# Batch 0 of the attention: first projection of batch 1 moved up behind unit 2 on its own signal, the plan of tiles moved to the end

## The chip, the cores and the metric

The kernel runs on one core of one Trainium2 chip. The metric is the device time of one execution in microseconds (us), median of several runs. TensorE, VectorE, ScalarE and GpSimd each work through a queue of instructions in the order in which they were written; SyncE issues most of the transfers. They meet only at semaphores: an instruction waits until a counter has reached a value. The profile calls the engines PE, DVE, ACT, POOL and SP.

## The reference, cut to what matters

```
xn  = layernorm(x)                                  # x: 16 batches of 512 tokens, 128 wide
q, k, v = xn@Wq, xn@Wk, xn@Wv                       # 16 heads, 8 wide
attn = softmax(causal(8 * l2norm(q) @ l2norm(k).T)) # per batch and head
attention = (attn @ v) @ Wo
probs = softmax(xn @ Wr.T); the 2 best of 8 experts, their shares made to sum to 1
ffn  = sum over the 2 of share * (gelu(xn @ W1[e].T + b1[e]) @ W2[e].T + b2[e])
out  = x + attention + ffn
```

## The kernel before

**Stages.** First every batch is normalised, turned and stored, and the experts of all tokens are chosen. Then the attention of batches 0 to 7 runs, then 71 tiles of the expert layer (each 256 tokens of one expert), then the attention of batches 8 to 15. GpSimd sends the rows of normalised tokens to their places in the experts' tiles (`slot_x`) with indirect transfers while the first eight batches run, and fetches the results during the later ones.

**One batch of attention.** `body` of TensorE goes through 12 units, k = 0 to 11. In unit k `scores` (L911 to L925) writes 1,536 columns of scores into one of two areas of PSUM, ScalarE raises them to exp (L813, one instruction each unit), GpSimd sets the masked ones to zero (`mask`, L666, one or two instructions in each unit), and `weigh` (L957, L968) multiplies the result by the values, in ten chunks c = 0 to 9. `scores` of unit k waits until the exp of unit k-2 is over, because it uses its area. `weigh` of chunk 0 starts the sums in PSUM bank 6 (`ps_o`); chunks 0 to 4 are the first half of the heads, chunks 5 to 9 the second. Between them VectorE must empty the bank: `evacuate` (L1361), then `divide` (L1367, L1371). Chunk 4 needs the masks of unit 6, chunk 6 those of unit 7, chunk 7 those of unit 9; the last two chunks follow in the next batch.

**Projections.** Among the units TensorE also makes q, k and v of the next batch, tile by tile: `project(b + 1, i)` (L883) for i = 0 to 3, all four into PSUM bank 7. VectorE takes each one out (`prepare`: `unload`, L1228 and L1235, then `halve`, L1244 to L1252), and `project` of the next tile waits for L1235 (the counter `proj_evac`). SyncE then turns each tile into place for the next batch's scores (L432).

**What is special in batch 0.** VectorE is still at work on the routing when batch 0 begins. From the ranks that TensorE left in bank 7 (`ps_pc`) it works out the slot of each token: L1326 and L1327 read the bank, L1328 to L1334 work on in SBUF, L1337 clears bank 6, and then it raises the counter `routed`. Three things wait for `routed`: `project(1, 0)`, because it overwrites bank 7; `weigh` of chunk 0, because of bank 6 and the buffers there; and GpSimd's first send. GpSimd's queue in batch 0 is written out by hand: masks of units 0 to 5, then a wait for `routed` and for the transfer that fills the last tiles with zeros (L625), one send, mask 6, two sends, mask 7, one send, mask 8, two sends, mask 9, one send, mask 10, one send, mask 11. VectorE in batch 0 prepares the four tiles of batch 1, then does `pick_tiles` (L1342 to L1345, the table of which expert owns which tile, needed by TensorE only in unit 7 of batch 1), then `evacuate` and `divide` of the first half.

The order of TensorE in batch 0: scores 0, 1, 2, 3; `project(1, 0)`; scores 4; chunks 0 and 1; scores 5; `project(1, 1)`; scores 6; chunk 2; `project(1, 2)`; scores 7, 8; chunk 3; `project(1, 3)`; chunk 4; scores 9, 10; chunks 5 and 6; scores 11; chunk 7.

Of the kernel before, what the change touches and what calls it, by code (L numbers as in the profile page):

```python
# [29 lines left out]
def build(nc, x, Wq, Wk, Wv, Wo, Wr, W1, b1, W2_, b2, out):  # L30
# [3 lines left out]
    TB = N // P  # L34
# [64 lines left out]
    with ExitStack() as ctx:  # L99
# [3 lines left out]
        def sem(name):  # L103
            return ctx.enter_context(nc.semaphore(name))

        def sems(names):
            return [sem(n) for n in names.split()]
# [145 lines left out]
        wtr_done, wt_ready, btr_done, bt_ready = sems("wtr_done wt_ready btr_done bt_ready")  # L253
        r_step, counted, totals_read, placed = sems("r_step counted totals_read placed")
        routed = sem("routed")
        residue_ready, later_ready = sems("residue_ready later_ready")
        gap_exp, = sems("gap_exp")
        pick_ready, picked, plan_ready = sems("pick_ready picked plan_ready")
# [13 lines left out]
        def some(count):  # L272


            return not isinstance(count, int) or count > 0
# [6 lines left out]
        def known(i, value):  # L282

            return isinstance(i, int) and i == value
# [5 lines left out]
        def tile_of(b, i):  # L290

            return i if known(b, 0) else TILE_AT[i]
# [542 lines left out]
        def _(pe):  # L835
# [35 lines left out]
            def project(b, i):  # L871

                t = tile_of(b, i)
                if i == 0:
                    pe.wait_ge(xt_in, 16 * (b + 1))
                if not known(b, 0):
                    if i == 0 and known(b, 1):
                        pe.wait_ge(routed, 1)
                    if i == 0 and some(b - 2):
                        pe.wait_ge(added, b - 2)  # L880
                    pe.wait_ge(proj_evac, TB * b + i)
                bank = psum[:, t, :] if known(b, 0) else psum[:, 7, :]
                pe.matmul(bank[:, 0:3 * D], xt[:, t * P:(t + 1) * P], wall[:, E:WEND], start=True, stop=True)\  # L883
                    .then_inc(proj_done, 1)
# [90 lines left out]
            def out_project(b, projected):  # L975
                pe.wait_ge(ot_ready, b + 1)
                pe.wait_ge(proj_evac, projected)
                for t in range(TB):
                    mm = pe.matmul(ps_out[:, t * D:(t + 1) * D], ot[:, t * P:(t + 1) * P], wo[:],  # L979
                                   start=True, stop=True)  # L980
                mm.then_inc(outp_done, 1)
# [34 lines left out]
            pe.wait_ge(bt_ready, 1)  # L1016
            pe.wait_ge(proj_evac, TB)

            def body(b, par, second=False, last=False):
                if known(b, HALF):  # L1020
                    pe.wait_ge(gelu_done, MC * FFN_TILES)
                    pe.wait_ge(ys_ready, FFN_TILES)
                fresh = known(b, 0) or known(b, HALF)
                for k in range(UN):
                    scores(b, par, k)
                    if k == 1 and not last and not known(b, 0):
                        project(b + 1, 0)
                    elif k == 2 and not fresh:
                        weigh(b - 1, 1 - par, 8)
                        weigh(b - 1, 1 - par, 9)  # L1030
                    elif k == 3 and not last:
                        project(b + 1, 0 if known(b, 0) else 1)
                    elif k == 4:
                        weigh(b, par, 0)
                        weigh(b, par, 1)
                    elif k == 5 and not last:
                        project(b + 1, 1 if known(b, 0) else 2)
                    elif k == 6:
                        weigh(b, par, 2)
                        if not last:  # L1040
                            project(b + 1, 2 if known(b, 0) else 3)
                    elif k == 7 and known(b, 1):
                        pe.wait_ge(pick_ready, 1)
                        pe.wait_ge(proj_evac, TB * (b + 2))
                        pe.matmul(ps_pick, pick[:], identh[:, 0:FFN_TILES], start=True, stop=True).then_inc(picked, 1)
                    elif k == 8:
                        weigh(b, par, 3)
                        if known(b, 0):
                            project(b + 1, 3)
                        weigh(b, par, 4)  # L1050
                    elif k == 9:
                        if known(b, 1):
                            pe.wait_ge(wo_in, 16 * 4 * QH)
                            pe.wait_ge(plan_ready, 1)
                        if not known(b, 0):
                            out_project(b - 1, TB * (b + 1) if last else TB * (b + 2))
                    elif k == 10:
                        weigh(b, par, 5)
                        weigh(b, par, 6)
                    elif k == 11:  # L1060
                        weigh(b, par, 7)
# [48 lines left out]
        def _(dve):  # L1110
# [91 lines left out]
            def next_step():  # L1202

                nonlocal steps
                steps += 1
                return steps
# [51 lines left out]
            def share_values(b, par):  # L1258

                if known(b, 0):  # L1260
                    dve.wait_ge(vp_made, 3)
                dve.wait_ge(proj_evac, TB * (b + 1))
                first = v[0:HP, par].rearrange("p (m j) x -> p j m x", j=2)[:, 0, :, 0:DH]
                dve.tensor_copy(vp[0:HP, par, :, 0:DH], first)
                other = v[0:HP, par].rearrange("p (m j) x -> p j m x", j=2)[:, 1, :, 0:DH]
                dve.tensor_copy(vp[HP:P, par, :, DH + 1:2 * DH + 1], other).then_inc(vp_ready, 1)
# [16 lines left out]
            def stepped(ins):  # L1283
                ins.then_inc(r_step, 1)
                dve.wait_ge(r_step, next_step())
# [38 lines left out]
            def of_halves(ap):  # L1324
                return ap.rearrange("p h (a e) -> p h a e", a=1).broadcast_to([P, 2, T // 2, E])
            dve.tensor_tensor(ahead, ranks, of_halves(upto[:, 1:3]), ALU.is_ge)  # L1326
            stepped(dve.tensor_tensor(at_rank, ranks, of_halves(begins[:, 0:2]), ALU.add))  # L1327
            stepped(dve.tensor_tensor(ahead, ahead, of_halves(jumps[:]), ALU.mult))  # L1328
            stepped(dve.tensor_tensor(at_rank, at_rank, ahead, ALU.add))
            for c in range(TOPK):  # L1330
# [10 lines left out]
            def pick_tiles():  # L1341
                stepped(dve.tensor_scalar(past[:], ends[:].rearrange("p c e -> p (c e)"), tile_at[:], None, ALU.is_le))  # L1342
                stepped(dve.tensor_tensor(past[:], past[:], weight[:], ALU.mult))
                stepped(dve.tensor_reduce(expert[:], past[:], AX.X, ALU.add))
                dve.tensor_scalar(pick[:], ones[:], expert[:], None, ALU.mult).then_inc(pick_ready, 1)  # L1345
# [60 lines left out]
            def body(b, par, second=False, last=False):  # L1406
                fresh = known(b, 0) or known(b, HALF)

                if known(b, 0):
                    share_values(0, 0)  # L1410
                if not (second or known(b, HALF)):
                    scale_of(b + 1, rnb[:])
                if not last:
                    prepare(b + 1, 1 - par, 0, second)
                if not fresh:
                    evacuate(b - 1, 1)
                if last:
                    divide(b - 1, 1)
                    turn_divided(b - 1)
                else:  # L1420
                    prepare(b + 1, 1 - par, 1, second)
                    if not fresh:
                        divide(b - 1, 1)
                    prepare(b + 1, 1 - par, 2, second)
                    if not fresh:
                        turn_divided(b - 1)
                    prepare(b + 1, 1 - par, 3, second)
                if known(b, 0):
                    pick_tiles()
                if known(b, 1):  # L1430
                    write_plan()
                evacuate(b, 0)
                divide(b, 0)
                if not last:
                    share_values(b + 1, 1 - par)
                if not known(b, 0):
                    add_attention(b - 1)
                if second and not known(b, HALF):
                    added_before = counted_by(dve, b)
                    dve.wait_ge(made, 1)  # L1440
                    dve.wait_ge(added, added_before)
                    combine(b - 1, 1 - par, range(MOVES))
                if last:
                    combine(b, par, range(2))
# [151 lines left out]
```

## Time and profile before

| | |
|---|---|
| time, median of 3 runs | 667.08 us (666.76 to 668.74) |
| the profiled execution: its own time | 667.76 us |
| its span, first to last instruction | 666.0 us |
| mean granted clock of TensorE | 0.971 of full speed |
| busy: TensorE, VectorE, ScalarE, GpSimd | 607.1, 461.8, 450.5, 427.2 us |

Times in the rows are microseconds from the start of the span; batch 0 lies between about 88 and 117. A row of the timeline gives start, duration, engine, line, operation, what it writes from what it reads, and in brackets how long the engine stood idle before it and what ended that.

### The profile page before, as it was taken

What the parts mean: (1) busy time and instruction counts of PE and PEld (TensorE: products, weight loads), DVE (VectorE), ACT (ScalarE), POOL (GpSimd) and SP (SyncE); (2) the same over time, 40 slices, a digit from 0 to 9 for tenths busy, and PEclk for the clock granted to TensorE, in tenths of its full rate; (3) what the DMA queues carried; (4) which work ended last, traced back from release to release, by engine and by line L of the source; (5) the groups of instructions that cost most, each with busy time, mean ns of one, the idle gap of its engine ahead of it and who ended that gap; (6) DMA issues with size and microseconds to landing.
All of it is one profiled execution on the core that took longest, in us unless ns stands there. A gap on an engine that the chain in (4) does not pass through costs nothing.

```text
span 666.0 us, 21498 instructions
## 1 busy us (share of the span) xinstructions
PE 607.1 (91%) x7417; PEld 411.3 (62%) x7417; DVE 461.8 (69%) x1296; ACT 450.5 (68%) x689; POOL 427.2 (64%) x617
## 2 busy tenths in 40 slices
PE   2877468999999989999999999999998999989985
PEld 2756322444444448999999999999994444434432
DVE  6799986677777776444444546777666688868846
ACT  3999546789898984444444444444457988978893
POOL 6356627778888887775600026777655777868773
PEclk9999868999999999999999999999999999989998
DMA  6997684445664568745332334444434466555541
GB/s 172 286 289 243 191 251 107 102 105 122 117 129 112 126 129 218 203 136 145 111 87 71 79 86 107 119 117 115 118 97 75 101 125 135 125 118 111 127 109 48
DMA packets 186593, 89.37 MB, mean 134 GB/s; under 512 B 115456, under 2 KB 176032, under 8 KB 186400
## 3 DMA queue, kind: packets, MB, share of 16 engines
q1 hardware_dynamic: 178192, 70.70, 43.8%
q0 software_dynamic: 8336, 17.84, 9.7%
q8 instruction: 36, 0.59, 0.4%
q14 instruction: 29, 0.24, 0.1%
HBM read 30.17 MB, written 32.24 MB: 94 GB/s over the span
## 4 chain that ended last, share of the span: by engine, by line
PE 74%; issue 4%; DVE 4%; ACT 4%; POOL 3%; DMA 2%; SPq 0%; DVEq 0%; ACTq 0%; POOLq 0%
PE psum L1085 19%; PE psum L1073 18%; PE psum L968 14%; PE psum L883 7%; PE psum L911 7%; ACT prob L813 2%; PE psum L918 2%; PE psum L957 2%; PE psum L979 2%; DMA xt<-xn_cols 2%; POOL prob L666 1%; PE psum L925 1%; POOL rows L650 1%; ACT prob L766 1%; POOL slot_x L652 1%
## 5 line engine op out<-in xcount | busy, mean ns | idle before, releaser
L813 ACT ACTIVATE prob<-psum 128x1536 f32<-128x1536 f32 x192 | 266.9, 1452 | 51.2 <-PE psum L911 47.7
L823 ACT ACTIVATE prob<-psum,prob 128x256 f32<-128x256 f32 x284 | 117.5, 471 | 132.9 <-PE psum L1073 130.1
L650 POOL DMA_INDIRECT rows<-slot_y,idx x128 | 131.4, 1026 | 45.9 <-issue 26.3
L652 POOL DMA_INDIRECT slot_x<-rows,slots x128 | 128.1, 1001 | 35.5 <-issue 29.4
L666 POOL TENSOR_SCALAR_AFFINE_SELECT prob<-prob 128x128 f32<-128x128 f32 (+2 forms) x256 | 112.8, 455 | 42.8 <-ACT prob L813 39.4
L1085 PEld LDWEIGHTS psum<-prob 128*128 128x128 f32 x1136 | 137.8, 192 | 3.6
L968 PE MATMUL psum<-prob,v 128*18 128x448 f32 (+3 forms) x2048 | 132.5, 388 | 7.9 <-POOL prob L666 7.7
L1085 PE MATMUL psum<-prob 128*128 128x128 f32 x1136 | 138.1, 275 | 0.0
L1073 PE MATMUL psum<-xs,prob 128*128 128x256 f32 x568 | 134.8, 380 | 0.9 <-DVE xs L1475 0.8
L1073 PEld LDWEIGHTS psum<-xs,prob 128*128 128x128 f32 x568 | 102.5, 190 | 12.8 <-issue 1.2
L968 PEld LDWEIGHTS psum<-prob,v 128*18 128x18 f32 x2048 | 50.4, 99 | 79.4 <-issue 57.9
L911 PE MATMUL psum<-qks 32*128 32x192 f16 (+3 forms) x1024 | 67.6, 275 | 4.3 <-ACT prob L813 4.1
L1482 DVE TENSOR_TENSOR xs<-psum,prob 128x256 f32<-128x256 f32 x71 | 30.1, 424 | 58.6 <-PE psum L1085 58.4
L883 PE MATMUL psum<-wall,xt 128*128 128x384 f32 x128 | 58.8, 544 | 4.0 <-issue 2.9
L911 PEld LDWEIGHTS psum<-qks 32*128 32x128 f16 x1024 | 20.7, 92 | 55.9 <-issue 25.4
L1459 DVE COPY prob<-wexp 128x516 f32 x71 | 31.6, 446 | 32.7 <-ACT prob L823 30.0
L1467 DVE COPY prob<-wexp 128x640 f32 x71 | 35.6, 502 | 14.6 <-DVE xs L1482 14.6
L635 POOL COPY idx<-slots 128x8 int32 (+1 forms) x16 | 3.5, 217 | 64.1 <-PE psum L1085 63.8
L1403 DVE SCALAR_TENSOR_TENSOR acc<-rows,gate,acc 128x128 f32<-128x128 f32 (+1 forms) x128 | 42.4, 395 | 3.0 <-DMA rows<-slot_y,idx 1.6
L1361 DVE STREAM_TRANSPOSE turn<-psum 128x512 f32<-128x512 f32 x31 | 22.2, 715 | 21.0 <-PE psum L968 21.0
L846 PE MATMUL psum<-wall,xts 128*128 128x264 f32 x128 | 32.0, 397 | 4.5 <-ACT logits L767 4.5
L1228 DVE TENSOR_TENSOR qn<-psum,rnb 128x256 f32<-128x256 f32 x36 | 14.8, 412 | 28.4 <-PE psum L883 28.3
(159 smaller groups left out, 676.5 us busy)
## 6 DMA issues: line engine op xcount, KB each, us to landing
slot_y<-xs SPq DMA_DIRECT2D x71, 128.0 KB
xs<-in_L_attn_x SPq DMA_DIRECT2D x16, 256.0 KB, 4.1
prob<-in_L_ffn_W SPq DMA_DIRECT2D x16, 256.0 KB, 3.6
xn_rows<-prob SPq DMA_DIRECT2D x16, 256.0 KB, 2.6
xn_cols<-xts SPq DMA_DIRECT2D x16, 256.0 KB, 3.0
xt<-xn_cols SPq DMA_DIRECT2D x16, 256.0 KB
rows<-xn_rows SPq DMA_DIRECT2D x16, 256.0 KB, 3.1
out<-acc SPq DMA_DIRECT2D x15, 256.0 KB
```

The costliest lines, as they stand in the source:

```text
L650: pool.indirect_dma_start(rows[:, j, c, t, :], None, done, where).then_inc(moved[j], 16)
L652: pool.indirect_dma_start(slot_x, where, halves_of_rows[:, j, 0, t, :], None).then_inc(moved[j], 16)
L666: pool.affine_select(out=p, in_=p, compare_op=ALU.is_ge, fill=0.0, base=HP, pattern=[[0, n], [0, 2], [1, HP]], channel_multiplier=-1).then ...
L813: act.activation(prob[:, KEPT[k], :], score[k % 2], ACT.Exp, scale=SCALE / UP ** 2)\
L823: act.activation(hs[:, s, c, :], psum[:, 2 * s + c // 2, (c % 2) * FT:(c % 2 + 1) * FT], ACT.Gelu, bias=ws[:, s, B1C + c:B1C + c + 1]).the ...
L883: pe.matmul(bank[:, 0:3 * D], xt[:, t * P:(t + 1) * P], wall[:, E:WEND], start=True, stop=True)\
L911: mm = pe.matmul(s[:, j * N + col:j * N + col + cols], keys, queries(qks[g:g + 32, par, 0, slab], kt, first, cols), start=True, stop=True)
L968: mm = pe.matmul(queries(ps_o[32 * g:32 * g + VW], kt, first, cols), pairs[par][:, kt * H // 2 + QH * o + g, odd:odd + VW], prob[:, KEPT[u ...
L1073: mm = pe.matmul(psum[:, 2 * s + c // 2, (c % 2) * FT:(c % 2 + 1) * FT], ws[:, s, c * P:(c + 1) * P], xgt[:, s, :], start=True, stop=True)
L1085: mm = pe.matmul(psum[:, 4 + s, j * D:(j + 1) * D], hs[:, s, c, j * P:(j + 1) * P], ws[:, s, W2C + c * D:W2C + (c + 1) * D], start=(c == 0 ...
L1403: dve.scalar_tensor_tensor(out=a, in0=r, scalar=gate[:, c, at(TB * m + t)], in1=a, op0=ALU.mult, op1=ALU.add).then_inc(combined, 1)
L1467: dve.tensor_copy(ws[:, s:s + 1, W2C:WX], wexp[:, at(e), W2C:WX]).then_inc(w2_ready, 1)
```

## The change

A second counter, `ranks_read`, is raised by VectorE as soon as L1327 has read bank 7; `project(1, 0)` waits for it in place of `routed`. In batch 0 TensorE follows a list of its own (`entry`): scores 0, 1, 2; `project(1, 0)`; scores 3, 4, 5; chunks 0 and 1; `project(1, 1)`; scores 6; chunk 2; `project(1, 2)`; scores 7, 8; `project(1, 3)`; chunks 3 and 4; scores 9, 10; chunks 5 and 6; scores 11; chunk 7. VectorE does `evacuate`, `divide` and `share_values` of batch 0 before `pick_tiles`. The same work is done; the queues of GpSimd, ScalarE and SyncE and the other batches keep their order.

```diff
+        ranks_read = sem("ranks_read")
...
                 if not known(b, 0):
                     if i == 0 and known(b, 1):
-                        pe.wait_ge(routed, 1)
+                        pe.wait_ge(ranks_read, 1)
...
+            def entry(k):
+
+                if k == 2:
+                    project(1, 0)
+                elif k == 5:
+                    weigh(0, 0, 0)
+                    weigh(0, 0, 1)
+                    project(1, 1)
+                elif k == 6:
+                    weigh(0, 0, 2)
+                    project(1, 2)
+                elif k == 8:
+                    project(1, 3)
+                    weigh(0, 0, 3)
+                    weigh(0, 0, 4)
+                elif k == 10:
+                    weigh(0, 0, 5)
+                    weigh(0, 0, 6)
+                elif k == 11:
+                    weigh(0, 0, 7)
...
                 for k in range(UN):
                     scores(b, par, k)
-                    if k == 1 and not last and not known(b, 0):
+                    if known(b, 0):
+                        entry(k)
+                        continue
+                    if k == 1 and not last:
                         project(b + 1, 0)
...
                     elif k == 3 and not last:
-                        project(b + 1, 0 if known(b, 0) else 1)
+                        project(b + 1, 1)
...
             stepped(dve.tensor_tensor(at_rank, ranks, of_halves(begins[:, 0:2]), ALU.add))
+            dve.sem_inc(ranks_read, 1)
             stepped(dve.tensor_tensor(ahead, ahead, of_halves(jumps[:]), ALU.mult))
...
-                if known(b, 0):
-                    pick_tiles()
                 if known(b, 1):
                     write_plan()
                 evacuate(b, 0)
                 divide(b, 0)
                 if not last:
                     share_values(b + 1, 1 - par)
-                if not known(b, 0):
+                if known(b, 0):
+                    pick_tiles()
+                else:
                     add_attention(b - 1)
```

## Rows read from the trace of the kernel before

**Rows 1.** The page: engines' busy time (us, share, instructions), and the chain that ended last.

```profile
PE 607.1 (91%) x7417; PEld 411.3 (62%) x7417; DVE 461.8 (69%) x1296; ACT 450.5 (68%) x689; POOL 427.2 (64%) x617
...
PE 74%; issue 4%; DVE 4%; ACT 4%; POOL 3%; DMA 2%; SPq 0%; DVEq 0%; ACTq 0%; POOLq 0%
```

**Rows 2.** Chain of waits in order of time: the first scores of batches 2 and 3.

```profile
136.90 0.54 PE psum L918 x2
...
155.22 0.54 PE psum L918 x2
```

**Rows 3.** Timeline of TensorE in batch 0.

```profile
93.67 0.39 PE L911 MATMUL psum<-qks 32*128 32x320 f16 x6 [1.10 <-ACT prob L813]
96.95 1.62 PE L883 MATMUL psum<-wall,xt 128*128 128x384 f32 x2 [2.89 <-issue]
...
101.97 0.91 PE L883 MATMUL psum<-wall,xt 128*128 128x384 f32 x2
...
107.35 1.06 PE L968 MATMUL psum<-prob,v 128*18 128x320 f32 x16
...
111.26 0.68 PE L957 MATMUL psum<-prob,xts 128*18 128x64 f32 x32 [2.31 <-DVE turn L1361]
...
114.78 1.91 PE L968 MATMUL psum<-prob,v 128*18 128x448 f32 x16 [0.59 <-POOL prob L666]
```

**Rows 4.** Timeline of ScalarE in batch 0.

```profile
90.67 5.63 ACT L813 ACTIVATE prob<-psum 128x1536 f32<-128x1536 f32 x4 [6.95 <-PE psum L911]
...
102.09 2.79 ACT L813 ACTIVATE prob<-psum 128x1536 f32<-128x1536 f32 x2 [1.48 <-PE psum L911]
```

**Rows 5.** Timeline of GpSimd in batch 0 and at the start of batch 1.

```profile
91.51 1.21 POOL L625 DMA_INDIRECT slot_x<-acc,pad_at  x1 [7.90 <-issue]
...
104.67 0.98 POOL L652 DMA_INDIRECT slot_x<-rows,slots  x1 [0.16 <-issue]
105.67 0.92 POOL L666 TENSOR_SCALAR_AFFINE_SELECT prob<-prob 128x256 f32<-128x256 f32 x2
...
111.74 1.16 POOL L652 DMA_INDIRECT slot_x<-rows,slots  x1 [0.17 <-ACT prob L813]
...
114.18 0.55 POOL L666 TENSOR_SCALAR_AFFINE_SELECT prob<-prob 128x384 f32<-128x384 f32 x1
...
120.34 0.29 POOL L666 TENSOR_SCALAR_AFFINE_SELECT prob<-prob 128x128 f32<-128x128 f32 x1 [2.19 <-ACT prob L813]
```

**Rows 6.** Timeline of VectorE in batch 0 and at the start of batch 1.

```profile
91.10 0.68 DVE L1327 TENSOR_TENSOR rows<-psum,begins 128x512 f32<-128x512 f32 x1
...
96.30 0.48 DVE L1337 MEMSET psum<- 128x512 f32 x1 [0.18 <-DVE slots L1334]
...
99.22 0.28 DVE L1235 COPY v<-psum 128x128 f32<-128x128 f32 x1
...
109.26 0.51 DVE L1342 TENSOR_SCALAR past<-ends,tile_at 128x24 f32<-128x24 f32 x1
...
110.51 0.70 DVE L1361 STREAM_TRANSPOSE turn<-psum 128x512 f32<-128x512 f32 x1
...
120.58 0.42 DVE L1228 TENSOR_TENSOR qn<-psum,rnb 128x256 f32<-128x256 f32 x1 [6.67 <-PE psum L883]
```

**Rows 7.** Transfers: packets between 83.2 and 88 us.

```profile
DMA packets 2243, 1.13 MB, mean 236 GB/s; under 512 B 1042, under 2 KB 2066, under 8 KB 2243
```

**Rows 8.** Transfers: the one that fills the last tiles, its time to landing (us) last.

```profile
slot_x<-acc,pad_at POOLq DMA_INDIRECT x1, 8.9
```

**Rows 9.** Stretches: busy time of each engine, PEclk the granted clock, DMA share, GB/s.

```profile
93.00:94.00 1.00, 0.33 (x6) 0.12 (x6) 0.93 (x3) 1.00 (x2) 0.64 (x2) 1.00 1.06 293
94.00:95.00 1.00, 0.06 (x3) 0.00 (x0) 0.96 (x2) 1.00 (x2) 0.11 (x1) 0.83 1.18 356
...
118.00:119.00 1.00, 1.00 (x26) 0.35 (x14) 0.00 (x0) 0.23 (x1) 0.15 (x1) 0.72 0.17 66
```

**Rows 10.** Stretches around the end of batch 7, same columns.

```profile
247.00:248.00 1.00, 0.00 (x0) 0.00 (x0) 0.00 (x0) 0.98 (x3) 0.97 (x1) 1.00 0.37 100
```

More of the change, by code:

```diff
@@ L1036, in body @@
                     elif k == 5 and not last:
-                        project(b + 1, 1 if known(b, 0) else 2)
+                        project(b + 1, 2)
                     elif k == 6:
@@ L1040, in body @@
                         if not last:
-                            project(b + 1, 2 if known(b, 0) else 3)
+                            project(b + 1, 3)
                     elif k == 7 and known(b, 1):
@@ L1047, in body @@
                         weigh(b, par, 3)
-                        if known(b, 0):
-                            project(b + 1, 3)
                         weigh(b, par, 4)
@@ L1054, in body @@
                             pe.wait_ge(plan_ready, 1)
-                        if not known(b, 0):
-                            out_project(b - 1, TB * (b + 1) if last else TB * (b + 2))
+                        out_project(b - 1, TB * (b + 1) if last else TB * (b + 2))
                     elif k == 10:
@@ L1427, in body @@
                     prepare(b + 1, 1 - par, 3, second)
-                if known(b, 0):
-                    pick_tiles()
                 if known(b, 1):
@@ L1435, in body @@
                     share_values(b + 1, 1 - par)
-                if not known(b, 0):
+                if known(b, 0):
+                    pick_tiles()
+                else:
                     add_attention(b - 1)
```

## The prediction

> **What bounds the kernel now.** I read the page first. TensorE is busy for 91% of the span, and 74% of the chain that ended last is its work [rows 1]. So the question is what ends batch 0 on TensorE, and whether time won there survives. The chain of waits shows how steady batches run: the first scores of batch 2 start at 136.90, those of batch 3 at 155.22, 18.32 us apart, with nothing but TensorE between them [rows 2].
>
> The timelines of batch 0 show four places where TensorE isn't the limit. It reaches scores 3 at 93.67, and then stands until 96.95, when `project(1, 0)` starts; the brackets count 2.89 us idle [rows 3]. L1337 ends at 96.30 + 0.48 = 96.78, and `routed` comes next: that is the wait [rows 6]. ScalarE runs four exps from 90.67 to 96.30, 1.41 us each, and then has nothing, because the scores of units 4 and 5 stand behind that wait; exps 5 and 6 run from 102.09 to 104.88 [rows 4]. GpSimd is late for the same reason: its first send starts at 104.67, mask 6 at 105.67, mask 9 at 114.18, and there is hardly a gap between; chunk 7 follows at 114.78, and the profile names L666 as its releaser [rows 3, 5]. Last, chunk 5 starts at 111.26, behind `evacuate`, though chunk 4 was over at 107.35 + 1.06 = 108.41 [rows 3]; between the two stood `pick_tiles`, from 109.26 to 110.51, 1.25 us [rows 6]. What ends batch 0 is GpSimd's queue, and what starts that queue late is exp 6, by way of `routed`.
>
> **The change step by step.** Times are those of the old profile up to 92 and worked out from there.
>
> *The first projection.* L1327 ends at 91.78 [rows 6], so the new signal is up at about 91.9. Scores 2 need exp 0 (92.08) and 0.4 us, so `project(1, 0)` starts at 92.5 and doesn't wait for VectorE. Nor for `xt`: its 128 pieces of 2 KB stand ahead of the load of `acc` in SyncE's queue, and 2243 - 2066 = 177 packets of 2 KB or more had passed by 88 us [rows 7]. One projection took 1.62 us at the low clock and 0.91 at the high one [rows 3]; here the clock is high [rows 9], so it ends at 93.4, before scores 3 could start (exp 1 ends at 93.49). It costs the path nothing. If `xt` came later, TensorE would stand in front of scores 3 to 5, and the old order would be back.
>
> *Units 3 to 5.* Their scores wait for exps 1, 2 and 3 (93.5, 94.9, 96.3) and take 0.4 us each [rows 3, 4]. Exps 4 and 5 then follow exp 3 without a gap, and exp 5 ends at 96.30 + 2 x 1.41 = 99.1, where it ended at 102.09 + 1.40 = 103.5 before. Chunks 0 and 1 wait for `routed`, still 96.9. The new signal stands in VectorE's queue ahead of it; no row has its price, which lies between nothing and 0.28, the shortest VectorE instruction in [rows 6]. I take 0.1.
>
> *The second projection is the new limit.* `project(1, 1)` waits for L1235 of tile 0. VectorE reaches that only after the routing and ended it at 99.50 [rows 6]; with the signal, 99.6. Chunks 0 and 1 are through by then: between 98.57 and 101.97 they and two units of scores took 3.40 us at the low clock [rows 3], so without the scores at most 2.6, from 97.0 to 99.6. From 99.6 the projection takes 0.91 or 1.62, scores 6 take 0.4 or, by estimate between that and its double, 0.6, and exp 6 takes 1.40: it ends at 102.3 at the high clock, 103.2 at the low one.
>
> *GpSimd.* Mask 5 follows exp 5 and is over at 100.0 (0.9 us for such a pair, as mask 6). Then GpSimd waits for the fill of the last tiles, issued at 91.51 and landed 8.9 us later, at 100.4 [rows 5, 8]; nothing of the change touches it. The first send (0.98) is over by 101.5, so mask 6 starts with exp 6, at 102.3 to 103.2 instead of 105.67: 3.4 or 2.5 us earlier. From mask 6 to mask 9 it took 114.18 - 105.67 = 8.51 us, the same instructions in the same order, and VectorE was at work beside them then as now. I keep 8.51; the upper bound is five sends at the 1.16 of the slowest one here in place of 0.98, 0.9 more [rows 5]. The Trainium skill speaks against the step here: by its page "SBUF — State Buffer", section "Who interferes with whom", a copy of VectorE in its fast modes shuts GpSimd out from writing the descriptors of a send until it is over. If each of the five sends waited out one copy of 0.28, that would be 1.4 us and the sum below 2.1; the rows agree with 0.18 a send at most. Exps 7 to 9 are in time: from `project(1, 1)` to the end of chunk 4 took 108.41 - 101.97 = 6.4 us [rows 3], so chunk 4 is over at 106.0 to 107.2 and exp 9, which needs its buffer, 1.4 us and a unit of scores later, before 109.1, when mask 9 is due at 110.8 or later. The swap of `project(1, 3)` and chunk 3 moves nothing past another engine's wait.
>
> *The plan of tiles.* Without `pick_tiles` ahead of it, `evacuate` starts up to 1.25 us sooner, around 107 to 108. That is worth nothing at the end, because chunk 7 still waits for mask 9 at 111 or later. Nor does `pick_tiles` cost anything at its new place: VectorE stands idle for 6.67 us before 120.58 [rows 6], and TensorE asks for the result in unit 7 of batch 1. Were that cover gone, it would cost its 1.25 us.
>
> *The clock after it.* Chunk 7 took 1.91 us at half speed, and the clock rose only about 118.5 (0.72 granted in 118 to 119) [rows 3, 9]. If it stays high this time, (118.5 - 114.8) / 2 = 1.9 us come on top; if it falls as before, nothing. TensorE will again stand for about 2 us before chunk 7, as it did for 2.31 before chunk 5, so I take 0.5, near the lower end. Against that, 247 to 248 was a whole microsecond without a matmul, at 1.00 granted [rows 10].
>
> *The sum.* 2.5 to 3.4 us earlier, of which I take 3.0, because TensorE between 93 and 97 is again busy for less than half of the time, and the last time that was so the clock fell inside 94 to 95 [rows 9]; and 0.5 from the clock after it: 3.5 us. It survives: batches 2 to 7 are TensorE's alone [rows 2], GpSimd had 2.19 us of slack at the start of batch 1 [rows 5], and all transfers of batch 1 start from semaphores that move along. The profiled execution took 667.76 us (its span 666.0), so the same one would take 664.3. It lies 0.68 above the median of the runs; from the median of 667.08 it is 663.6, which I give.
>
> **The rivals.** *The clock stays high.* The trace speaks half for it: high at 247 in spite of the gap [rows 10], low from 94 on although scores ran until then [rows 9]. Then mask 6 starts 3.4 us earlier and the tail gives 1.9: 5.3 us, 661.8. [...]
>
> *The gain goes on GpSimd's queue: no change.* The sends stretch, or the fill lands later. Five slow sends (0.9) and the low clock leave 2.5 - 0.9 = 1.6 us: 665.5. For nothing at all, the first send would have to start at 104.67 as before, the fill 4.3 us later than it landed. Against it: sends ran beside a busy VectorE before too.
>
> *Slower, by the clock.* Many short gaps between 93 and 99.6 could keep TensorE at 1.2 GHz where the second projection of the old order already ran at 2.4 (0.91 at 101.97) [rows 3], and again behind chunk 7. A microsecond on TensorE's path at half speed costs 0.5. To use up 3.0 and lose 2.0 more, the low stretches must be 10 us longer than before: low until about 107 and again until 122. Then 669.5. Nothing in the trace lasts so long while TensorE is as busy as from 99.6 on.
>
> **How the numbers follow.** 0.3% of 667 is 2.0 us, about what a measurement of this kernel can tell from no change. The forecast, a gain of 2.0 to 4.6 us, gets 0.59; the high clock 0.15; no change 0.19; slower 0.07. Faster is 0.59 + 0.15 = 0.74, same 0.19, slower 0.07. The forecast's own range is 662.5 to 665.1. The range down to 661.3 takes in the high clock with half a microsecond to spare; up to 666.3 it takes in the stretched sends. What is left out is a gain of under 0.8 us and a loss.
>
> **What would show it.** The first projection should start at 92.5 and scores 3 at 93.5; six exps should run on end from 90.67 to 99.1; `project(1, 1)` should start at 99.6, released by VectorE's L1235; mask 6 should start at 102.3 to 103.2, and chunk 7 at 110.8 to 112.3 with GpSimd still its releaser; the first scores of batch 2 should come 3 to 4 us before 136.90. I am wrong if `project(1, 0)` waits for something else, if mask 6 waits for a send or the fill rather than for exp 6, or if the granted clock is low for longer in sum than before.

## The result and the profile after

The changed kernel takes 665.47 us (median of 20 runs, 663.35 to 668.51); the kernel before took 668.35 on the same chips (20 runs, 666.42 to 672.33). The ratio is 0.9947, 95% interval 0.9931 to 0.9963: faster by 0.53%, or 3.5 us of 668.35, where 3.5 us were forecast; the medians themselves lie 2.9 apart. 665.47 lies 1.9 above the forecast time of 663.6, and 1.3 of that are the kernel before itself, which took 668.35 here and 667.08 in the three runs that the forecast started from.

The profiled execution took 666.04 us, its span is 664.3. Its times can't be set beside those of before as they stand, since this execution came to batch 0 about a microsecond later. As a common mark I take the first matmul of the counts on the routing, which no edit touches: it starts at 87.18 here and started at 86.20 before (L1006 there). "After the mark" is a time less that start. TensorE's timeline in batch 0 of the changed kernel (the lines of the file have moved: `project` is L884, scores L912 to L926, chunks L958 and L969):

```profile
87.18 0.27 PE L1007 MATMUL psum<-residue,xs 128*128 128x8 f16 x4 [0.78 <-DVE xs L1301]
...
92.57 0.39 PE L912 MATMUL psum<-qks 32*128 32x448 f16 x6 [0.62 <-ACT prob L814]
92.92 0.89 PE L884 MATMUL psum<-wall,xt 128*128 128x384 f32 x2
...
96.60 0.41 PE L912 MATMUL psum<-qks 32*128 32x320 f16 x6 [0.95 <-ACT prob L814]
99.02 1.06 PE L958 MATMUL psum<-prob,xts 128*18 128x64 f32 x32 [2.01 <-DVE xts L1288]
...
101.72 1.65 PE L884 MATMUL psum<-wall,xt 128*128 128x384 f32 x2
...
110.16 0.64 PE L958 MATMUL psum<-prob,xts 128*18 128x64 f32 x32 [0.45 <-DVE turn L1384]
...
114.36 1.91 PE L969 MATMUL psum<-prob,v 128*18 128x448 f32 x16 [2.37 <-POOL prob L667]
116.21 1.03 PE L919 MATMUL psum<-barred,identh 128*128 128x512 f16 x2
```

ScalarE's timeline of the same stretch, and GpSimd's:

```profile
91.06 8.17 ACT L814 ACTIVATE prob<-psum 128x1536 f32<-128x1536 f32 x6 [6.35 <-PE psum L912]
103.90 1.45 ACT L814 ACTIVATE prob<-psum 128x1536 f32<-128x1536 f32 x1 [4.67 <-PE psum L912]
```

```profile
92.50 1.21 POOL L626 DMA_INDIRECT slot_x<-acc,pad_at  x1 [7.91 <-issue]
...
101.54 1.01 POOL L653 DMA_INDIRECT slot_x<-rows,slots  x1 [1.51 <-issue]
105.49 0.66 POOL L667 TENSOR_SCALAR_AFFINE_SELECT prob<-prob 128x256 f32<-128x256 f32 x2 [2.95 <-ACT prob L814]
...
113.75 0.56 POOL L667 TENSOR_SCALAR_AFFINE_SELECT prob<-prob 128x384 f32<-128x384 f32 x1
...
119.59 0.29 POOL L667 TENSOR_SCALAR_AFFINE_SELECT prob<-prob 128x128 f32<-128x128 f32 x1 [1.85 <-ACT prob L814]
```

VectorE's:

```profile
92.92 0.69 DVE L1351 TENSOR_TENSOR logits<-logits,jumps 128x512 f32<-128x512 f32 x1 [0.16 <-DVE rows L1349]
...
97.41 0.48 DVE L1360 MEMSET psum<- 128x512 f32 x1 [0.18 <-DVE slots L1357]
...
98.59 0.29 DVE L1288 COPY xts<-v 64x256 f32<-64x256 f32 x1
...
100.50 0.28 DVE L1257 COPY v<-psum 128x128 f32<-128x128 f32 x1
...
111.82 0.24 DVE L1365 TENSOR_SCALAR past<-ends,tile_at 128x24 f32<-128x24 f32 x1
...
119.83 0.42 DVE L1250 TENSOR_TENSOR qn<-psum,rnb 128x256 f32<-128x256 f32 x1 [5.93 <-PE psum L884]
```

And stretches of a microsecond (the busy time of TensorE is the second figure, the granted clock the third from the end):

```profile
95.00:96.00 1.00, 0.39 (x6) 0.12 (x6) 0.93 (x3) 1.00 (x2) 0.76 (x2) 1.00 1.07 293
96.00:97.00 1.00, 0.40 (x6) 0.12 (x6) 0.97 (x2) 1.00 (x2) 0.33 (x1) 0.92 1.12 369
97.00:98.00 1.00, 0.01 (x1) 0.00 (x0) 0.71 (x2) 1.00 (x2) 0.21 (x1) 0.50 1.01 420
...
103.00:104.00 1.00, 1.00 (x11) 0.27 (x14) 0.60 (x3) 0.10 (x1) 0.00 (x0) 0.66 0.86 192
...
117.00:118.00 1.00, 1.00 (x38) 0.58 (x38) 0.00 (x0) 0.00 (x0) 0.72 (x2) 0.84 0.19 70
```

The first projection starts at 92.92, 5.74 after the mark in place of 10.75 [rows 3], and six exps run on end from 91.06. But chunk 0 starts only at 99.02, 2.01 us idle behind L1288, the copy that shares out the values; L1360, behind which `routed` is raised, had ended at 97.89. The clock has fallen in 96 to 97 and the second projection takes 1.65 us, from 101.72. So exp 6 starts at 103.90, mask 6 at 105.49, mask 9 at 113.75, chunk 7 at 114.36, and GpSimd is its releaser as before [rows 3, 5]. After the mark, mask 6 moved from 19.47 to 18.31, chunk 7 from 28.58 to 27.18 and the first scores of batch 1 from 30.43 to 29.03: 1.40 us. The low clock ends at about 117.3, 30.1 after the mark where it was 32.4, and the first scores of batch 2 come 1.7 us earlier.

### The profile page after: what moved, and what is told of

The parts are those of the page before. It is cut to its first block, busy times and chain, and to the rows that moved or that the text cites. A ratio compares the mean times of both kernels' runs of the same rounds, so it can differ in the third digit from the quotient of the medians.

```text
span 664.3 us, 21499 instructions
## 1 busy us (share of the span) xinstructions
PE 605.6 (91%) x7417; PEld 411.8 (62%) x7417; DVE 460.8 (69%) x1296; ACT 450.2 (68%) x689; POOL 428.0 (64%) x617
## 4 chain that ended last, share of the span: by engine, by line
PE 73%; DVE 6%; issue 4%; ACT 3%; POOL 3%; DMA 1%; SPq 0%; DVEq 0%; ACTq 0%; POOLq 0%
PE psum L1107 19%; PE psum L1095 18%; PE psum L969 15%; PE psum L884 7%; PE psum L912 6%; ACT prob L814 2%; PE psum L919 2%; PE psum L958 2%; PE psum L980 2%; POOL prob L667 2%; PE psum L926 1%; POOL rows L651 1%; DMA xt<-xn_cols 1%; POOL slot_x L653 1%; ACT prob L767 1%
## 5 line engine op out<-in xcount | busy, mean ns | idle before, releaser
L969 PE MATMUL psum<-prob,v 128*18 128x448 f32 (+3 forms) x2048 | 130.7, 385 | 9.7 <-POOL prob L667 9.5
L969 PEld LDWEIGHTS psum<-prob,v 128*18 128x18 f32 x2048 | 50.1, 98 | 79.8 <-issue 53.3
L912 PE MATMUL psum<-qks 32*128 32x320 f16 (+3 forms) x1024 | 66.7, 273 | 5.6 <-ACT prob L814 5.2
L1505 DVE TENSOR_TENSOR xs<-psum,prob 128x256 f32<-128x256 f32 x71 | 30.1, 424 | 58.8 <-PE psum L1107 58.7
L884 PE MATMUL psum<-wall,xt 128*128 128x384 f32 x128 | 58.5, 541 | 1.3 <-DMA xt<-xn_cols 0.6
L912 PEld LDWEIGHTS psum<-qks 32*128 32x128 f16 x1024 | 20.6, 92 | 57.0 <-ACT prob L814 25.0
L597 POOL TENSOR_TENSOR rows<-prob 128x512 f32<-128x512 f32 x16 | 20.6, 1288 | 21.3 <-DVE xns L1200 19.6
```

The costliest lines, as they stand in the source:

```text
L912: mm = pe.matmul(s[:, j * N + col:j * N + col + cols], keys, queries(qks[g:g + 32, par, 0, slab], kt, first, cols), start=True, stop=True)
L969: mm = pe.matmul(queries(ps_o[32 * g:32 * g + VW], kt, first, cols), pairs[par][:, kt * H // 2 + QH * o + g, odd:odd + VW], prob[:, KEPT[u ...
```

## The experiments

Each ratio is to the kernel before, on the same chip; its median there lay between 668.35 and 669.35, so rows are compared by their ratios and not by their medians. To keep what happens in batch 0 apart from what happens later, the table gives, for the profiled execution of each, the starts of the first scores of batch 1 and batch 2 after the mark.

| kernel | median, us | ratio (95%) | batch 1 | batch 2 |
|---|---|---|---|---|
| before | 668.35 | 1 | 30.43 | 50.63 |
| changed | 665.47 | 0.9947 (0.9931 to 0.9963) | 29.03 | 48.92 |
| changed, old signal | 669.16 | 0.9990 (0.9972 to 1.0009) | 31.32 | 51.00 |
| changed, plan of tiles first | 666.04 | 0.9956 (0.9934 to 0.9979) | 27.67 | 47.33 |
| before, new signal alone | 665.76 | 0.9961 (0.9937 to 0.9986) | 29.23 | 48.63 |
| changed, sends spread | 661.01 | 0.9884 (0.9849 to 0.9919) | 25.47 | 45.13 |
| before, sends spread | 666.62 | 0.9950 (0.9933 to 0.9967) | 29.46 | 48.85 |
| changed, values shared early | 663.70 | 0.9921 (0.9894 to 0.9947) | 27.47 | 47.38 |
| the same, fillers in front | 665.63 | 0.9939 (0.9916 to 0.9963) | 27.57 | 47.95 |
| changed, fillers at the end | 664.14 | 0.9916 (0.9892 to 0.9940) | 28.40 | 48.08 |
| changed, sends spread, values early | 663.96 | 0.9927 (0.9902 to 0.9952) | 24.92 | 44.61 |
| before, signal, sends spread | 664.98 | 0.9948 (0.9927 to 0.9969) | 28.33 | 47.86 |

**The old signal in the new order.**

```diff
-                        pe.wait_ge(ranks_read, 1)
+                        pe.wait_ge(routed, 1)
```

> The changed kernel, but the first projection waits for the old signal again; the new order of TensorE and the late plan of tiles stay. Theory (the gain is the early signal): the first projection starts near 97 again, now with the scores of units 3 to 5 all behind it, and exp 6 ends 1 to 2 us later than in the kernel before; the whole gain goes, 668 to 671 us, ratio to the kernel before 1.000 to 1.004. Rival (the gain comes from the order or from the plan of tiles): it stays near 0.995.

The time is that of the kernel before: the gain is gone. The ratio lies just under the 1.000 to 1.004 expected, which its interval reaches into. TensorE's timeline of this run:

```profile
97.57 1.62 PE L884 MATMUL psum<-wall,xt 128*128 128x384 f32 x2 [4.50 <-issue]
...
104.52 1.65 PE L884 MATMUL psum<-wall,xt 128*128 128x384 f32 x2
...
117.03 1.06 PE L969 MATMUL psum<-prob,v 128*18 128x448 f32 x16 [2.37 <-POOL prob L667]
```

TensorE stands for 4.50 us in front of the first projection, and the second starts 17.82 after the mark in place of 15.77 before. In this execution the new order without the early signal is worse than the old one, by 0.9 us at batch 1; by the ratio the two can't be told apart. The new order and the late plan together don't make the gain without the signal.

**The plan of tiles first, as before.**

```diff
+                if known(b, 0):
+                    pick_tiles()
                 if known(b, 1):
                     write_plan()
                 evacuate(b, 0)
...
-                if known(b, 0):
-                    pick_tiles()
-                else:
+                if not known(b, 0):
                     add_attention(b - 1)
```

> The changed kernel, but the plan of tiles stands ahead of the emptying of the first half again, as before. Theory (GpSimd's mask 9 ends batch 0): chunk 5 starts up to 1.25 us later, chunk 7 does not, and the time is that of the changed kernel, ratio 0.995 within 0.0015. Rival (the first half emptied sooner is what gains): 1.25 us of the 2.9 go, ratio 0.9966 or more.

0.9956 against 0.9947: nothing that can be told from the changed kernel, though the interval takes in the rival's 0.9966 too. TensorE's timeline decides between them, and shows something else:

```profile
110.32 0.64 PE L958 MATMUL psum<-prob,xts 128*18 128x64 f32 x32 [1.45 <-DVE turn L1384]
...
113.28 1.06 PE L969 MATMUL psum<-prob,v 128*18 128x448 f32 x16 [1.14 <-POOL prob L667]
114.28 0.61 PE L919 MATMUL psum<-barred,identh 128*128 128x512 f16 x2
```

Chunk 5 waits 1.45 us for `evacuate` where it waited 0.45 in the changed kernel, and chunk 7 still waits for GpSimd behind it, 1.14 us. So the 1.0 us lost at chunk 5 is not lost at chunk 7. But chunk 7 takes 1.06 us here and 1.91 there: in this execution the clock stayed high. That is 0.85 of the 1.36 us by which its batch 1 starts earlier in the table; for the other 0.51 GpSimd's mask 9 came earlier, 26.07 after the mark in place of 26.57. Whether the clock stayed high because the plan cuts one wait of 2.37 us into two shorter ones, or by chance, is not shown: with the old signal it stayed high behind an uncut 2.37.

**The signal alone.** The kernel before with `ranks_read` raised behind L1327 and awaited by the first projection, all else old.

```diff
-                        pe.wait_ge(routed, 1)
+                        pe.wait_ge(ranks_read, 1)
...
             stepped(dve.tensor_tensor(at_rank, ranks, of_halves(begins[:, 0:2]), ALU.add))
+            dve.sem_inc(ranks_read, 1)
```

> The kernel before with the new signal alone: the first projection still behind unit 3, the old order after it, the plan of tiles first. Theory, by the trace after (chunk 0 waits for the shared values at about 97.6 and runs at the low clock): scores 5 come after chunks 0 and 1, exp 6 ends near 104.5 in place of 104.88 and mask 6 starts with it, 1.2 us earlier than 105.67; a gain of 0.5 to 2 us, ratio 0.997 to 0.999. Rival 1 (the signal is all of it): 0.995. Rival 2 (without the new order it is worth nothing): 1.000.

0.9961, with batch 1 at 29.23: within the measurement the whole change. TensorE's timeline, and GpSimd's mask 9:

```profile
111.22 0.64 PE L958 MATMUL psum<-prob,xts 128*18 128x64 f32 x32 [2.79 <-DVE turn L1363]
...
113.82 1.80 PE L969 MATMUL psum<-prob,v 128*18 128x448 f32 x16
```

```profile
112.87 0.55 POOL L667 TENSOR_SCALAR_AFFINE_SELECT prob<-prob 128x384 f32<-128x384 f32 x1
```

Mask 9 starts 26.54 after the mark, as early as in the changed kernel (26.57), so by these two executions the signal alone brings GpSimd's queue all that the change brings it there. But chunk 7 no longer waits for it: it follows scores 11 without a gap, and what ends batch 0 here is chunk 5, 2.79 us idle behind `evacuate`, which stands behind the plan of tiles. The size of the gain, 2.6 us by the ratio, is above what I expected by mask 6 alone (GpSimd's mask 6 starts at 104.81, 18.48 after the mark, 1.0 earlier than before). The interval reaches from 0.9937 to 0.9986 and so doesn't shut the expectation out.

**GpSimd's sends spread out.** Two sends behind mask 5, then one behind each mask: three sends and not five between masks 6 and 9.

```diff
-                        order = [[], [], [], [], [], [0], [1, 2], [3], [4, 5], [6], [7], []]
+                        order = [[], [], [], [], [], [0, 1], [2], [3], [4], [5], [6], [7]]
```

> The changed kernel with GpSimd's sends of batch 0 spread otherwise: two behind mask 5, then one behind each mask, so that three sends and not five lie between mask 6 and mask 9. Theory (GpSimd's queue ends batch 0): mask 9 and chunk 7 come about 2.4 us earlier, TensorE has almost no gap before chunk 7 and keeps the high clock there: 2 to 4 us below the changed kernel, ratio to the kernel before 0.989 to 0.992. Rival (chunk 7 is held by TensorE or ScalarE as well): 0.5 us or less below the changed kernel, ratio 0.994 or more.

0.9884: 1.2% below the kernel before, more than twice what the change brought. The timelines of GpSimd and TensorE in this run:

```profile
102.08 0.96 POOL L653 DMA_INDIRECT slot_x<-rows,slots  x1 [0.31 <-issue]
104.76 0.66 POOL L667 TENSOR_SCALAR_AFFINE_SELECT prob<-prob 128x256 f32<-128x256 f32 x2 [1.71 <-ACT prob L814]
...
110.44 0.56 POOL L667 TENSOR_SCALAR_AFFINE_SELECT prob<-prob 128x384 f32<-128x384 f32 x1
```

```profile
110.71 0.40 PE L912 MATMUL psum<-qks 32*128 32x320 f16 x6
111.05 1.06 PE L969 MATMUL psum<-prob,v 128*18 128x448 f32 x16
```

Mask 6 starts 18.14 after the mark, about as in the changed kernel (18.31), but mask 9 at 23.82 in place of 26.57. Chunk 7 starts right behind scores 11, without a wait, at the high clock; batch 1 starts 3.6 us earlier than in the changed kernel, and batch 2 3.8. The ratio lies just under the 0.989 expected; its interval (0.9849 to 0.9919) reaches into the expected range and stays clear of the changed kernel's.

**The same spread in the kernel before**, with nothing else changed (the same line).

> The kernel before with nothing changed but GpSimd's sends of batch 0 spread out (two behind mask 5, then one behind each mask). Theory (in the kernel before TensorE was late as well: scores 11 ended at 114.2, 0.6 us before chunk 7 started): mask 9 comes over 2 us earlier, but chunk 7 only 0.6 us, ratio 0.998 to 1.000. Rival (GpSimd's queue alone ended batch 0 before the change too): 2 to 2.5 us, ratio 0.9965 or less.

By the median time the rival is right, 0.9950; by the trace the theory is, as far as chunk 7 goes: scores 11 and chunk 7 follow each other without a wait,

```profile
97.25 1.62 PE L883 MATMUL psum<-wall,xt 128*128 128x384 f32 x2 [2.78 <-issue]
...
111.62 0.64 PE L957 MATMUL psum<-prob,xts 128*18 128x64 f32 x32 [1.96 <-DVE turn L1361]
...
113.74 0.61 PE L911 MATMUL psum<-qks 32*128 32x320 f16 x6
114.28 1.74 PE L968 MATMUL psum<-prob,v 128*18 128x448 f32 x16
```

chunk 7 starts 27.78 after the mark in place of 28.58, 0.8 us, and batch 2 starts 1.8 us earlier, because the low clock ends sooner as well. The ratio stands for 3.3 us; 1.7 of it are in front of the expert tiles of this execution (164.28 and 162.54 after the mark), the rest isn't accounted for by one trace. As with the signal alone, chunk 5 waits for `evacuate` (1.96 us) and nothing behind it waits for GpSimd: in the old order TensorE was late by nearly as much as GpSimd.

**The values shared early.** `share_values(0, 0)` moved from the first line of VectorE's batch 0 to the 0.6 us in which it waits for TensorE's counts.

```diff
+            share_values(0, 0)
             dve.wait_ge(counted, 1)
             dve.tensor_copy(totals.rearrange("p c n -> p (c n)"), ps_o).then_inc(totals_read, 1)
...
-                if known(b, 0):
-                    share_values(0, 0)
```

> The changed kernel, but VectorE shares out the values of batch 0 (which chunk 0 needs) earlier, in the 0.6 us in which it waits for TensorE's counts, and not behind the routing. Theory (in the changed kernel chunk 0 is held by the shared values, a wait that the prediction left out): chunk 0 starts 0.7 to 0.9 us earlier, the second projection and mask 6 follow, and the time falls by about 0.8 us, ratio to the kernel before 0.992 to 0.995. Rival (the routing or the second projection's own wait holds it): as the changed kernel, 0.9947 or more.

0.9921, batch 1 1.56 us earlier than in the changed kernel. Timelines of TensorE and GpSimd:

```profile
96.99 0.64 PE L958 MATMUL psum<-prob,xts 128*18 128x64 f32 x32 [0.48 <-issue]
...
99.05 1.65 PE L884 MATMUL psum<-wall,xt 128*128 128x384 f32 x2
```

```profile
101.64 1.23 POOL L653 DMA_INDIRECT slot_x<-rows,slots  x1 [1.84 <-issue]
102.89 0.66 POOL L667 TENSOR_SCALAR_AFFINE_SELECT prob<-prob 128x256 f32<-128x256 f32 x2
```

Chunk 0 starts 10.87 after the mark in place of 11.84. The other 0.6 of the 1.56 us are the clock's: chunks 0 and 1 take 2.06 us to the start of the second projection, where they took 2.70, since the clock falls only in 97 to 98 here (0.86 granted). The next limit shows: the first send waits 1.84 us for the fill of the last tiles and ends at 102.87, and exp 6 ends at 101.29 + 1.45 = 102.74; mask 6 starts behind both, so by these times an earlier exp 6 alone would win nothing more.

**Fillers in front.** As the run before, and four matmuls of 512 columns ahead of the scores of units 3, 4 and 5, into the area that these overwrite: more work for TensorE, to keep its clock up.

```diff
                 s = score[k % 2]
+                if known(b, 0) and k in (3, 4, 5):
+                    for _ in range(4):
+                        pe.matmul(s[:, 0:N], identh[:], ..., start=True, stop=True)
```

> As the run with the values shared early, and TensorE fills its gaps in units 3 to 5 of batch 0 with four matmuls of 512 columns ahead of each unit's scores, into the area that these scores then overwrite (extra work, nothing left out). Theory (the low clock from about 97 on costs the second projection 1.5 to 2 us): the granted clock stays at 1.00 through chunks 0 and 1, exp 6 ends 2 to 2.7 us earlier than in the changed kernel, ratio to the kernel before 0.990 to 0.993. Rival (the clock falls all the same, or the fillers push the scores back): no better than with the values shared early, 0.993 or more.

No gain shows: 0.9939 against 0.9921 without the fillers, with intervals that overlap. The clock was 1.00 from 97 to 113, and the second projection took 0.91 us; but it was still low when the first fillers came,

```profile
94.60 1.80 PE L905 MATMUL psum<-barred,identh 128*128 128x512 f16 x4
...
101.01 0.91 PE L884 MATMUL psum<-wall,xt 128*128 128x384 f32 x2
```

four of them took 1.80 us, the scores of units 3 to 5 came late, and batch 1 starts where it does without fillers (27.57 and 27.47). The run without them had its clock at 1.00 from 91 to 97, this one at 0.50 until 96, so the two timelines differ by more than the fillers. That a high clock there would gain 2 us is not shown.

**Fillers at the end.** Eight matmuls of 512 columns into bank 7 between scores 11 and chunk 7 of the changed kernel.

```diff
                 elif k == 11:
+                    pe.wait_ge(proj_evac, 2 * TB)
+                    for _ in range(8):
+                        pe.matmul(psum[:, 7, :], identh[:], ..., start=True, stop=True)
                     weigh(0, 0, 7)
```

> The changed kernel with eight matmuls of 512 columns into bank 7 (free by then) between scores 11 and chunk 7 of batch 0: extra work of 1.7 us at the high clock in a gap of about 2.4 us. Theory (the clock falls in this gap in some executions and then makes chunk 7 and the first scores of batch 1 slow): the clock stays at 1.00, chunk 7 starts when it did, and 0.5 to 1.5 us are won, ratio to the kernel before 0.992 to 0.994. Rival (the clock there costs nothing because GpSimd or ScalarE holds batch 1): 0.9947. Where the fillers end after mask 9, it would be slower than the changed kernel by up to 0.5 us.

```profile
112.16 1.90 PE L1041 MATMUL psum<-barred,identh 128*128 128x512 f16 x8
114.59 1.06 PE L969 MATMUL psum<-prob,v 128*18 128x448 f32 x16 [0.54 <-POOL prob L667]
```

In this timeline the fillers fill the gap, the wait for GpSimd is down to 0.54 us, chunk 7 takes 1.06 us and batch 2 starts 0.84 us earlier than in the changed kernel. The ratio, 0.9916, agrees with the theory, but its interval (0.9892 to 0.9940) overlaps that of the changed kernel.

**Both that paid.** Sends spread and values shared early.

> The changed kernel with both of what paid: the sends of batch 0 spread out and the values of batch 0 shared early. Theory (the waits stand in one row: shared values, second projection, exp 6, GpSimd): chunk 0 starts about 1 us earlier than with the sends spread alone, but the two sends ahead of mask 6 now wait for the fill of the last tiles, so mask 6 gains only 0.3 to 0.7 us; ratio to the kernel before 0.985 to 0.989, at or just below the sends alone (0.9884). Rival (the two gains add): 0.9884 less the 0.0026 between the run with early values and the changed kernel, 0.986 or less. Rival 2 (the fill takes all): 0.9884 or more.

Batch 1 starts 0.55 us earlier than with the sends alone (24.92 and 25.47), as the theory has it: the first send waits 1.46 us for the fill. The ratio of 0.9927 misses the expected 0.985 to 0.989. It lies above the 0.9884 of the sends alone, but the two come from separate sets of runs with intervals that overlap, and the executions of either kernel differ by more than this step (661.24 to 665.86 us here). That the gains add, 0.986, lies outside the interval, and nothing shows that the second one is worth keeping beside the first.

**The sends spread with the signal alone**, in the old order and with the plan of tiles first.

> The kernel before with the new signal and the sends of batch 0 spread out; the old order of TensorE (first projection behind unit 3, scores 5 behind chunks 0 and 1) and the plan of tiles ahead of the emptying stay. Theory (the new order and the late plan were hidden behind GpSimd's queue in the change; with the queue out of the way they pay): exp 5 and with it the first two sends come 3 us later than in the changed kernel with sends spread, chunk 5 waits for the plan of tiles, and the time is 2 to 3 us above that run: ratio 0.991 to 0.9935. Rival (order and plan are worth nothing here either): 0.9884.

```profile
110.24 0.64 PE L958 MATMUL psum<-prob,xts 128*18 128x64 f32 x32 [1.98 <-DVE turn L1363]
...
112.53 1.91 PE L969 MATMUL psum<-prob,v 128*18 128x448 f32 x16
```

0.9948, a little above the range expected, and batch 1 at 28.33: 2.9 us behind the changed kernel with the same sends (25.47). Here the new order and the late plan do pay: exp 5 ends late again, mask 5 starts 16.61 after the mark in place of 13.03, and chunk 5 waits 1.98 us for `evacuate`. Chunk 5 starts 24.19 after the mark in place of 22.66, 1.5 us later; the rest of the 2.9 lies behind it, where chunk 7 takes 1.91 us at the low clock in place of 1.06. Which of the two parts carries how much wasn't taken apart.

## Why the prediction was right, and where it was not

*That the first projection starts at 92.5 and holds nothing up: right.* 5.74 after the mark; 6.3 were forecast (92.5 less 86.2). The 0.6 that it comes earlier are chance: the exps start 3.88 after the mark in place of 4.47, as the clock was granted in full from about 90 in this execution, 2.8 after the mark, and before from about 91.3, 5.1 after it. The signal cost VectorE 0.16 us of idle time behind L1349, where I took 0.1. With the old signal in the new order the gain was gone, so the signal is the cause, shown by itself (0.9990) and by the run with it alone (0.9961).

*That six exps run on end: right*, from 91.06 to 99.23.

*That the second projection's wait for L1235 is the new limit: wrong, and this is the step that was mis-sized.* I had chunks 0 and 1 start with `routed` and be through before 99.6, 13.4 after the mark. Chunk 0 has a third wait, for the shared values (`vp_ready`), which I left out, here and in the description of batch 0: VectorE makes them behind the routing, so chunk 0 started 1.13 us after the end of L1360. Before the change this wait was hidden behind the first projection. At the low clock the two chunks then took 2.7 us, and the second projection started 14.54 after the mark, when L1257 (L1235 before) had been over for 0.94 us. Moving the copies forward won back 0.97 us at chunk 0.

*That mask 6 gains 2.5 to 3.4 us: too much.* It gained 1.16 in this execution. The clock was low, for which 2.5 had been forecast; less the 1.14 by which the second projection was late, and 0.14 between the end of exp 6 (105.35) and the mask, that is 1.2. (The 107.2 given there for the end of chunk 4 should be 106.9 by its own terms; nothing hangs on it.)

*That GpSimd's queue from mask 6 to mask 9 keeps its 8.51 us and ends batch 0: right.* 113.75 - 105.49 = 8.26, the sends of it took 0.96 to 1.07 us, and chunk 7's releaser is the mask. That it ends batch 0 holds for the changed kernel; before, TensorE was ready for chunk 7 only 0.59 us ahead of the mask [rows 3], and with the sends spread in the kernel before, or with the signal alone, TensorE was the later of the two. By the Trainium skill's page "SBUF — State Buffer", section "Who interferes with whom", copies of VectorE in its fast modes can hold these sends up. The longest send in the lines shown here took 1.23 us, and sends with VectorE idle beside them took 0.97, so the traces show at most 0.26 of it a send, and 0.10 in these five.

*That the plan of tiles is worth nothing: right* as the changed kernel stands (0.9956 and 0.9947, and chunk 7 waiting for GpSimd either way); with the signal alone chunk 5 waits 2.79 us behind it and ends batch 0.

*That 0.5 us come from the clock behind it: right in kind.* Chunk 7 was slow again in the profiled execution, but the low stretch ended 2.2 us earlier after the mark, of which 1.4 are the shift itself. In the run with the plan first it stayed high.

*The sum.* In the profiled pair batches 0 and 1 give 1.7 us, not 3.5, and that lasts: the expert tiles start 1.7 us earlier after the mark (162.58 and 164.28). The spans differ by 1.7 too, but as 1.7, another 1.0 won in the second half, and 1.0 lost ahead of the mark. The median gain is 2.9 and the ratio stands for 3.5, so other executions gained more than this one. What the missing 1 to 2 us are stays open. The clock differs from one execution to the next, but only the profiled execution's clock is on record stretch by stretch, and the mean granted clock of the 20 executions speaks against it as the whole cause: the seven at 0.979 took 663.35 to 663.84 us, the six at 0.981 or 0.982, the profiled one among them, 665.8 to 666.3. So the agreement of 3.5 with 3.5 is in part luck: of the forecast's two terms, 3.0 and 0.5, the first measured 1.2 at mask 6 in the one execution that can be followed.

*The rival of a high clock* didn't come about in the first half of batch 0: the clock fell in 96 to 97, with TensorE busy for 0.39 of the microsecond from 95 to 96 and for 0.40 of that in which it fell. *No change through GpSimd's queue*: the fill held the first send for 1.51 us, until 101.54, but mask 6 waited for exp 6. *Slower by the clock* was not seen: from the mark to the end of the low clock behind chunk 7 it was low for about 13 us in sum, before for about 19.

## What to carry to other kernels

When a wait is taken away, list every counter that the instructions behind it wait for, and when each is raised: a wait hidden by the old one is the next limit, and here it took a microsecond of a forecast gain of 3. Where an engine's queue is what ends a stage, its own order is worth looking at before the signals that feed it: moving two sends out from in front of a mask gained as much by itself as the whole change, and 3.6 us more on top of it by the start of batch 1. And parts that are worth nothing behind one limit, as the order and the plan of tiles were, can pay once that limit is gone.

## What the runs showed of the hardware

The same gap can leave the clock high or low. In the second half of the kernel TensorE waits 2.10 us for GpSimd in the same place of the program in both kernels; before the change the first line below, after it the second (TensorE's timelines):

```profile
586.49 1.91 PE L968 MATMUL psum<-prob,v 128*18 128x448 f32 x16 [2.10 <-POOL prob L666]
```

```profile
586.25 1.06 PE L969 MATMUL psum<-prob,v 128*18 128x448 f32 x16 [2.10 <-POOL prob L667]
```

The same chunk of 16 matmuls took 1.91 us at the low clock and 1.06 at the high one. The 2.37 us in front of chunk 7 of batch 0 did the same: the chunk took 1.91 us in the changed kernel and 1.06 with the old signal. From the first scores of batch 9 to those of batch 13, where the wait of 2.10 us lies, the kernel took 78.1 us before and 77.3 after, and nothing in that stretch was changed.
